# Token MLP after an NNMF convolution: the variances of an image pair gathered in one PSUM bank, their inverse root taken once a pair, and the orders of all engines written anew

## What is computed

```python
def token_mlp(x, h, g2, b2, w_fc1, b_fc1, w_fc2, b_fc2):
    y = x + h
    mu = mean(y, channels)
    var = mean((y - mu) ** 2, channels)
    yn = (y - mu) * rsqrt(var + 1e-5) * g2 + b2
    z = gelu(yn @ w_fc1 + b_fc1)      # 96 -> 384
    return y + z @ w_fc2 + b_fc2      # 384 -> 96
```

## Time and profile before

| | |
|---|---|
| median of 3 runs | 6704.27 us (6704.2 to 6706.16) |
| the profiled execution | 6705.41 us, of which its span is 6703.6 us |
| TensorE, VectorE, ScalarE, GpSimd busy | 90%, 82%, 57%, 71% of the span |
| mean granted TensorE clock | 0.981 |
| first and last load of the logarithm's table | 6174.4 us and 6660.1 us |

### The profile page before, as it was taken

How to read it: one execution, slowest core, us unless ns; L and a number is a source line. 1 busy time by engine, 2 the same in 40 slices (tenths; PEclk the granted TensorE clock), 3 DMA queues, 4 the chain that set the end, 5 groups by cost and what they waited for, 6 DMA issues and landing times. The chain is left out here.

```text
span 6703.6 us, 228614 instructions
## 1 busy us (share of the span) xinstructions
PE 6053.1 (90%) x96819; PEld 3479.4 (52%) x96819; DVE 5507.3 (82%) x8016; ACT 3811.1 (57%) x5690; POOL 4761.0 (71%) x3268
## 2 busy tenths in 40 slices
PE   7999999999779999999999999999999999996877
PEld 3444444444345555555555555655555665553333
DVE  5776776776578888888888888888888888886998
ACT  3444444444346666656666655666665666664776
POOL 2344333334258888888888888888888888886766
PEclk9999999999889999999999999999999999998999
DMA  1111111111100000010000010000001000001221
GB/s 30 43 46 41 53 43 46 46 42 47 34 26 3 3 3 3 3 44 3 3 3 3 3 35 13 3 3 3 3 3 44 3 3 3 3 3 50 71 75 52
DMA packets 115654, 157.60 MB, mean 24 GB/s; under 512 B 30512, under 2 KB 79952, under 8 KB 114768
## 3 DMA queue, kind: packets, MB, share of 16 engines
q1 hardware_dynamic: 114768, 144.38, 7.6%
HBM read 53.67 MB, written 52.79 MB: 16 GB/s over the span
## 5 line engine op out<-in xcount | busy, mean ns | idle before, releaser
L241 ACT ACTIVATE nn_yy<-nn_P 128x612 f32<-128x612 f32 x1200 | 817.0, 681 | 1656.8 <-DVE nn_P L330 1639.3
L397 PE MATMUL nn_P<-nn_hh,nn_w 64*64 64x256 f16 x38400 | 1534.8, 273 | 220.6 <-DVE nn_nl L341 107.1
L209 POOL TENSOR_TENSOR nn_hf<-nn_hf,nn_sr 128x512 f32<-128x512 f32 (+1 forms) x800 | 1439.9, 1821 | 155.4 <-DVE nn_sr L363 155.4
L220 POOL TENSOR_TENSOR nn_hl<-nn_hf,nn_hh 128x512 f16<-128x512 f32 (+1 forms) x768 | 1266.2, 1649 | 314.5 <-ACT nn_hh L253 306.3
L397 PEld LDWEIGHTS nn_P<-nn_hh,nn_w 64*64 64x64 f16 x38400 | 1022.7, 106 | 834.0 <-issue 664.7
L404 PE MATMUL nn_P<-nn_nh,nn_w 64*64 64x512 f16 x19200 | 1320.6, 379 | 77.6 <-DVE nn_nl L341 8.8
L330 DVE SCALAR_TENSOR_TENSOR nn_P<-nn_P,nn_xs 128x612 f32<-128x612 f32 x1200 | 960.4, 800 | 234.2 <-PE nn_P L397 209.6
L336 DVE TENSOR_TENSOR nn_P<-nn_P,nn_nh 128x612 f32<-128x612 f32 x1200 | 960.2, 800 | 213.2 <-ACT nn_nh L246 206.8
L397 PE MATMUL nn_P<-nn_hl,nn_w 64*64 64x256 f16 x19200 | 994.0, 270 | 1.5 <-issue 1.2
L341 DVE SCALAR_TENSOR_TENSOR nn_nl<-nn_P,nn_nh 128x612 f16<-128x612 f32 x1200 | 952.1, 793 | 34.3
L246 ACT ACTIVATE nn_nh<-nn_yy 128x612 f16<-128x612 f32 x1200 | 856.1, 713 | 37.9
(11 more groups left out here) (215 smaller groups left out, 7986.1 us busy)
## 6 DMA issues: line engine op xcount, KB each, us to landing
xn_scratch<-at_xb SPq DMA_DIRECT2D x128, 114.8 KB
nn_xs<-xn_scratch SPq DMA_DIRECT2D x48, 306.0 KB, 3.0
at_x<-in_x SPq DMA_DIRECT2D x32, 384.0 KB, 3.8
x_scratch<-at_x SPq DMA_DIRECT2D x64, 192.0 KB, 2.1
h_scratch<-nn_hf SPq DMA_DIRECT2D x48, 256.0 KB, 3.1
ml_xt<-x_scratch SPq DMA_DIRECT2D x32, 384.0 KB, 4.4
ml_ht<-h_scratch SPq DMA_DIRECT2D x128, 96.0 KB
out<-ml_ot SPq DMA_DIRECT2D x64, 192.0 KB, 2.1
```

The lines of the kernel that those rows point to most:

```text
L209: e.tensor_tensor(hf[c][:, g, :], hf[c][:, g, :], sr[c][:, :].unsqueeze(1).broadcast_to((128, g.stop - g.start, A_COLS)), ALU.mult).then_i ...
L220: e.tensor_tensor(hl[c][:, g, :], hf[c][:, g, :], hh[c][:, g, :], ALU.subtract).then_inc(h_lo[n], 1)
L241: e.activation(half(yy[k % RING][:, :]), Pv[k % 2], ACT.Ln).then_inc(logged, 1)
L397: return pe.matmul(out[:, 0:AC, rows_y] if near else out[:, 1:BC, rows_y], w1[rows, wp, a, 1 if near else 0, k, cols], (hh, hl)[dp][u][row ...
```

## The change

- The variances of the four units of a pair go to one PSUM bank. `mean_w` has four forms of 96x128, form u with 1/96 in columns 32u to 32u + 31 and zero elsewhere, and the four matmuls of a pair accumulate: rows 32u to 32u + 31 of `PV` hold the variance of unit u. The semaphore counts once a pair.
- `log_var`, `inv_root`, `var_a`, `var_b` and `refine_root` run once a pair, on 128 rows.
- A new operation `spread` (TensorE, four a pair) multiplies the root by `pick`, which has a one in row 32u for all 96 columns: PSUM tile `PS` then holds unit u's root on 96 rows.
- `square` has a second instruction ahead of it: ScalarE copies the centred values from PSUM to an SBUF tile `xc`. `scale` reads `PS` and `xc` in place of `PX_` and `vr`, and waits for the spread and the square; `centring` waits for the square of two units ago, no longer for its scale.
- The orders of all five engines are new. Step n works on pairs n to n - 3, six steps are unrolled at the front and five at the end.
- In `nnmf` the two semaphores `pe_go` and `pool_go` become one, `go`.

```diff
-        centre = sb("centre", [CH, CH]); mean_w = sb("mean_w", [CH, CH]); eps_c = sb("eps_c", [CH, 1])
+        centre = sb("centre", [CH, CH]); mean_w = sb("mean_w", [CH, UNITS, 128]); pick = sb("pick", [128, UNITS, CH]); eps_c = sb("eps_c", [128, 1])
...
+        xc = [sb(f"xc{i}", [CH, HALF]) for i in range(4)]
+        vl = sb("vl", [128, HALF]); vy = sb("vy", [128, HALF])
+        va = sb("va", [128, HALF]); vb = sb("vb", [128, HALF]); vr = sb("vr", [128, HALF])
...
-        PV = [ctx.enter_context(nc.psum_tensor(f"ml_PV{i}", [128, 512], F32)) for i in (0, 1)]
+        PV = ctx.enter_context(nc.psum_tensor("ml_PV", [128, 512], F32))
+        PS = ctx.enter_context(nc.psum_tensor("ml_PS", [128, 512], F32))
...
-        AHEAD = 2
+        AHEAD = 3
...
             def square(b, p, t, u):
                 need(e, s_centred, UNITS * b + u + 1)
-                need(e, s_var, UNITS * b + u - 3)
+                need(e, s_yn, UNITS * b + u - 3)
+                e.activation(xc[u][:, :], PX_[u % 2][0:CH, :], ACT.Copy)
+                need(e, s_var, b)
                 e.activation(sqr[u][:, :], PX_[u % 2][0:CH, :], ACT.Square).then_inc(s_sqr, 1)
...
+            def log_var(b, p, t):
+                need(e, s_vy, b)
+                need(e, s_var, b + 1)
+                e.activation(vl[:, :], PV[:, :], ACT.Ln, bias=eps_c[:, :]).then_inc(s_vl, 1)
...
             def scale(b, p, t, u):
-                need(e, s_vr, UNITS * b + u + 1)
+                need(e, s_spread, UNITS * b + u + 1)
+                need(e, s_sqr, UNITS * b + u + 1)
                 need(e, s_yn_lo, UNITS * b + u - 3)
-                e.scalar_tensor_tensor(yn[u][:, :], PX_[u % 2][0:CH, :], -0.5, vr[:, :], ALU.mult, ALU.mult).then_inc(s_yn, 1)
+                e.scalar_tensor_tensor(yn[u][:, :], PS[0:CH, :], -0.5, xc[u][:, :], ALU.mult, ALU.mult).then_inc(s_yn, 1)
...
             def centring(b, p, t, u):
                 need(e, s_y, 2 * b + u // 2 + 1)
-                need(e, s_yn, UNITS * b + u - 1)
+                need(e, s_sqr, UNITS * b + u - 1)
...
             def variance(b, p, t, u):
                 need(e, s_sqr, UNITS * b + u + 1)
-                need(e, s_vab, 2 * (UNITS * b + u) - 3)
-                e.matmul(PV[u % 2][0:CH, :], mean_w[:, :], sqr[u][:, :], start=True, stop=True).then_inc(s_var, 1)
+                if u == 0:
+                    need(e, s_vab, 2 * b - 1)
+                mm = e.matmul(PV[:, :], mean_w[:, u, :], sqr[u][:, :], start=u == 0, stop=u == UNITS - 1)
+                if u == UNITS - 1:
+                    mm.then_inc(s_var, 1)
+
+            @only
+            def spread(b, p, t, u):
+                need(e, s_vr, b + 1)
+                need(e, s_yn, UNITS * b + u)
+                e.matmul(PS[0:CH, :], pick[:, u, :], vr[:, :], start=True, stop=True).then_inc(s_spread, 1)
...
-                e.sem_inc(pool_go, 1)
+                e.sem_inc(go, 1)
```

More of the change, by code:

```diff
@@ L413, in recon_near @@
                         need(e, h_lo[n], count(it, 1, 1))
-                e.sem_inc(pe_go, 1)
+                e.sem_inc(go, 1)
                 for a, wp, dp in COMBOS:
@@ L1293, in token_mlp @@
         s_vr = ctx.enter_context(nc.semaphore("ml_vr"))
+        s_spread = ctx.enter_context(nc.semaphore("ml_spread"))
         s_prepared = ctx.enter_context(nc.semaphore("ml_prepared"))
@@ L1320, in token_mlp @@
         flat = lambda ap: ap.rearrange("(a n) -> a n", n=1)
-        AHEAD = 2
+        AHEAD = 3
         def pairs(e, step):
-            first = 4
+            first = 6
             for n in range(first):
@@ L1370, in step @@
             def step(n, p, t):
-                store(pair(n, p, t, 2), 3)
                 load((n + 2, p, t + 1)) if not isinstance(n, int) or n + 2 < B else None
-                store(pair(n, p, t, 1), 0)
-                store(pair(n, p, t, 1), 1)
-                store(pair(n, p, t, 1), 2)
+                for u in range(UNITS):
+                    store(pair(n, p, t, 2), u)
             load((0, 0, 0))
@@ L1398, in step @@
             def step(n, p, t):
[L1399 to L1402, removed]
+                b0, b1, b2, = pair(n, p, t, 0), pair(n, p, t, 1), pair(n, p, t, 2)
+                g_low(b2, 0, 1); y_low(b2, 2); g_low(b2, 0, 2); g_low(b2, 1, 0); g_low(b2, 1, 1); y_low(b2, 3); g_low(b2, 1, 2)
+                g_low(b2, 2, 0); g_low(b2, 2, 1); g_low(b2, 2, 2); g_low(b2, 3, 0); g_low(b2, 3, 1); g_low(b2, 3, 2); y_low(b1, 0)
+                y_low(b1, 1); g_low(b1, 0, 0)
             pairs(e, step)
@@ L1454, in step @@
             def step(n, p, t):
[L1455 to L1460, removed]
+                b0, b1, b2, b3, = pair(n, p, t, 0), pair(n, p, t, 1), pair(n, p, t, 2), pair(n, p, t, 3)
+                gelu(b3, 3, 0); gelu(b3, 3, 1); gelu(b3, 3, 2); square(b2, 3); norm_table(b2); log_var(b2); inv_root(b2); copy_h(b1, 1, 0)
+                gelu_table(b2); y_high(b2, 0); square(b1, 0); copy_h(b1, 1, 1); gelu(b2, 0, 0); y_high(b2, 1); gelu(b2, 0, 1)
+                square(b1, 1); copy_h(b0, 0, 0); gelu(b2, 0, 2); y_high(b2, 2); copy_h(b0, 0, 1); gelu(b2, 1, 0); gelu(b2, 1, 1)
+                gelu(b2, 1, 2); gelu(b2, 2, 0); y_high(b2, 3); square(b1, 2); gelu(b2, 2, 1); gelu(b2, 2, 2)
             pairs(e, step)
@@ L1525, in step @@
             def step(n, p, t):
[L1526 to L1532, removed]
+                b0, b1, b2, b3, = pair(n, p, t, 0), pair(n, p, t, 1), pair(n, p, t, 2), pair(n, p, t, 3)
+                g_high(b3, 3, 1); result(b3, 1); g_high(b3, 3, 2); residual(b1, 0); var_a(b2); var_b(b2); refine_root(b2); result(b3, 2)
+                scale(b2, 0); result(b3, 3); scale(b2, 1); residual(b1, 1); g_high(b2, 0, 0); g_high(b2, 0, 1); scale(b2, 2)
+                g_high(b2, 0, 2); g_high(b2, 1, 0); g_high(b2, 1, 1); scale(b2, 3); g_high(b2, 1, 2); g_high(b2, 2, 0); g_high(b2, 2, 1)
+                result(b2, 0); g_high(b2, 2, 2); g_high(b2, 3, 0)
             pairs(e, step)
@@ L1573, in step @@
             def step(n, p, t):
[L1574 to L1578, removed]
+                b0, b1, b2, b3, = pair(n, p, t, 0), pair(n, p, t, 1), pair(n, p, t, 2), pair(n, p, t, 3)
+                centring(b2, 3); widen(b3, 1, 2); widen(b3, 2, 0); widen(b3, 2, 1); widen(b3, 2, 2); narrow(b3, 0); widen(b3, 3, 0)
+                widen(b3, 3, 1); variance(b2, 1); widen(b3, 3, 2); narrow(b3, 1); variance(b2, 2); variance(b2, 3); narrow(b3, 2)
+                centring(b1, 0); centring(b1, 1); spread(b2, 0); narrow(b3, 3); spread(b2, 1); widen(b2, 0, 0); widen(b2, 0, 1)
+                spread(b2, 2); widen(b2, 0, 2); variance(b1, 0); centring(b1, 2); spread(b2, 3); widen(b2, 1, 0); widen(b2, 1, 1)
             pairs(e, step)
```

58 lines of the change are left out of this document (28 added, 30 removed).

## The result

The changed kernel takes **6630.99 us** (median of 4 runs, 6629.1 to 6632.33) against 6705.22 us of the kernel before in the same comparison: ratio 0.9888, 95% interval 0.9871 to 0.9905. It was forecast at 6640 us, 6618 to 6678. The profiled execution took 6629.98 us, its span is 6628.2 us.

A forecast was written before the change was run, and what follows sets the result against it. It took mutual exclusion of VectorE's SBUF-only operations and GpSimd's as the bound: 31.1 to 27.0 us a pair, 32.38 to 28.2 at 96% use; fifteen intervals save 63, head and tail make 65, from 6704.3 to 6640 us, range 6618 to 6678.

The forecast's parts named there:

- the sum: Last stage: shared-resource time per pair at 96% use, over fifteen intervals 63 us saved, with head and tail 65.
- The interval: Last stage, time of one pair between table loads: from 32.38 to 28.2 us.
- the common resource: Last stage, what VectorE's SBUF-only operations and GpSimd's exclude each other from: 31.1 us a pair falls to 27.0.
- more than counted: Rival, last stage: fewer blockings, TensorE's 26.1 us sets a pair of 27.2, kernel 6624 us; chance 0.09.
- over 75% busy: Sign for the forecast: GpSimd's busy share after the change.
- The lists: Engine queues in the last stage: nothing in the new orders ends last, so no cost.
- slower: Rival, last stage: root chain and a blocking wholly outside TensorE's work, 34.9 us a pair, kernel 6741; chance 0.04.
- The chain and its cover: Fourth variance to first `widen`: 6.7 us, covered by 6.6 us of other TensorE work, costed at nothing.
- Durations: Changed last-stage operations at lower bounds: spread 0.86 us, copy 0.58, `scale` 0.68, refinement on 128 rows no longer.
- Head and tail: Before the first and behind the last table load: head some 4 us later, tail some 6 shorter, together -2.
- The clock: TensorE's granted clock of 0.92 would rise, said within the rival of chance 0.09.
- The lock: Ports shared by VectorE and GpSimd: whoever starts first holds them exclusively for the whole instruction.

The follow-up runs named there:

- b_short: Kernel before, with `var_b` and `refine_root` of units 1 to 3 on 8 of their 512 columns: 31.33 us a pair, after 32.38.
- b_order_short: b_order with `var_b` and `refine_root` of units 1 to 3 on 8 of their 512 columns: 29.28 us a pair, after 29.31.
- a_order: Changed kernel with operations in its lists moved once more, no new operation: 26.69 us a pair, after 27.87; kernel ratio 0.9871.
- a_order_port6: a_order with six more VectorE multiplications of 96x512 SBUF tiles a pair: 28.81 us a pair, after 26.69.
- b_order: Kernel before, every operation unchanged, only the five engine lists written anew: 29.31 us a pair, after 32.38; kernel ratio 0.9925.
- Both doses: Changed kernel with six more VectorE multiplications a pair, or separately with each spread issued twice: 30.51 and 30.31 us a pair, after 27.87.
- a_oldorder2: Changed kernel's operations in lists like those of before, SyncE's included: 40.21 us a pair, against 32.38 before; kernel ratio 1.0186.
- b_centre2: Kernel before with each centring matmul issued twice into the same bank: 32.59 us a pair, after 32.38.

## Why the prediction was right, and where it was not

- **The time**: 65 us were forecast, 66.6 came in the stage. The other 8 us of the measured 74 lie in the stages ahead, within the spread that they show from kernel to kernel; the sum has no term for them. That the stage came out so near to the forecast is luck, as the next points show.
- **The interval**: 28.2 forecast (27.0 / 0.96 is 28.1), 27.87 measured. The number is right and the reason given for it is not. The step that failed is "the common resource falls from 31.1 to 27.0 us; at the same 96% use a pair takes 28.2". b_short removed 3.2 of those 4.1 us and gained 1.05; b_order_short removed as much from better lists and gained 0.03; a_order runs a pair in 26.69, under the 27.0 that the sum calls for, and a_order_port6 in 28.81 with 31.1. The stretched durations were rightly read as blocking, but I took blocking that the old lists produced for a need of the work. b_order shows it as that: 62 us of VectorE's busy time go with no instruction removed. The sum also counts each instruction whole: in the earlier trace rows a blocked `refine_root` of 0.68 us ended only 0.56 behind the GpSimd instruction that held it up.
- **What sets the pace after**: TensorE, which was the rival "more than counted", at 0.09. Its work is 25.9 us at the full clock, 93% of the 27.87: 72 x 0.216 (nine `narrow` matmuls from 6346.99 to 6348.94 in the timeline above) + 12 x 0.86. It was counted as 26.1, with 0.22 for an fp16 matmul (the 4.12 / 18 of the earlier trace rows is 0.23, so 0.22 was no upper bound). Both doses cost about the same, so VectorE with GpSimd stands close behind. GpSimd was to be over 75% busy and is 73%.
- **The lists** were costed at nothing, as a carrier of the change. Of 4.51 us a pair, 3.07 are to be had by lists alone, and the rest came only with the changed operations and their lists together: those operations in lists like the old ones cost 7.8 us. This was the part to look at first. The rival "slower" named the mechanism (the chain outside TensorE's work) but 34.9 us a pair was too low a price: a_oldorder2 took 40.21. It left out that the clock was lower after such a wait (0.50, with a spread of 2.02 us, after 3.71 idle) and that every spread then waits for its scale; how the 5.3 us divide between the two was not tried.
- **The chain and its cover**, 6.7 against 6.6 us, costed at nothing: nearly right, 0.4 us uncovered in the pair shown.
- **Durations**: spread 0.86, copy 0.58, `scale` 0.68, refinement on 128 rows 0.69 for `refine_root` and 0.69 to 0.94 for `var_b`, where GpSimd was in the way. Unblocked, all lie at the lower bound that was taken.
- **Head and tail**: +4 forecast for the head, 6.6 measured; -6 for the tail, -5.6 measured.
- **The clock**: the rival said it would rise; it rose from 0.92 to 1.00, and in b_order as well. It has no term in the sum, where it is worth something: in b_centre2 TensorE's other work took 2.1 us a pair less at 0.99 than at 0.92.
- **The lock**: the Trainium skill (SBUF — State Buffer, the section on its two separate sides) puts the shared ports under an exclusive lock, which a VectorE instruction with two inputs in SBUF contends for. The rows agree in that `scale`, with one operand in PSUM, took 0.67 to 0.69 us in all 64 cases. It also has the lock held for the whole instruction, and by whole durations the sum came out too large: a_order_port6 would need 31.1 us in a pair of 28.81.

## What to carry to other kernels

A busy engine whose instructions stretch is not proof of a bound: take the suspected work away in the old order before believing that its removal pays, and compare with a kernel in which only the order changes. Merging small operations into one per group makes one long chain out of several short ones; here it paid where the order laid other work over that chain, and made the stage 23% longer where it did not. Compare stages, not whole kernels, when the gain is near the spread of what runs ahead.

## What the runs showed of the hardware that I had not expected

- Matmuls that do nothing can be nearly free: 3.4 us more of TensorE a pair cost 0.21 us, with the granted clock of the stretch at 0.99 in place of 0.92.
- A short instruction can wait as well: `refine_root` on 8 columns takes 0.15 us at least and 0.49 in the mean of b_short.
- VectorE's operations on 128 rows take as long as on 96: 0.69 us against 0.68, and fp32 matmuls over 128 rows as long as over 96, 0.87 us (spread) and 0.86 (centring).
- Stages that no edit touched moved by 14.5 us between kernels: with the NNMF the same to the letter, the last stage began at 6138.6 us in b_short and at 6153.1 in the kernel before.
